# Attention scores in full precision on four row groups, units in pairs, in a four-batch layer on one core

## The chip, the cores and the metric

The kernel runs on one NeuronCore of a Trainium2 chip. TensorE (PE in the profile) multiplies matrices and writes to PSUM; VectorE (DVE), ScalarE (ACT) and GpSimd (POOL) do the elementwise work; SyncE (SP) issues DMAs. Each engine runs its own instructions in program order, and the engines wait for each other by semaphores. The metric is the device time of one execution in microseconds, lower is better.

## The reference, cut to what matters

x is 4 batches of 512 tokens by 256 features. Each batch goes through a conditioned down/up projection with a residual (h), an attention over 8 heads, and a gated expert layer behind a second conditioned projection. The attention is what the change touches:

```
paths = sigmoid(h @ Wp + bp)                    # 512 x 8 heads x 5 levels
agree = pq * pk + (1 - pq) * (1 - pk)           # query, key
sim   = cumprod(agree, -1).sum(-1) / 5
attn  = softmax(where(causal, sim, -inf), -1)
ctx   = attn @ (h @ Wv);   out = ctx @ Wo
x     = x + out
x     = x + ffn(cond2(x))                       # argmax over 8 experts, each a 256 x 256 matrix
```

With s = tanh(logit / 2) for a path's sign, the sum of running products is an inner product of 32 features per token and head (all 32 products of subsets of the 5 levels, each scaled by a constant). So a head's score is a matmul with a contraction of 32.

## The kernel before, in words

Everything is held transposed: features in partitions, tokens along the free axis. The order of all work is one list, ORDER. Each engine walks the same list and issues its own part of each step, so the list sets the order on every queue. A step that uses a PSUM bank gets one from `work` (two banks in the loop, six in the prologue, four of them borrowed from `s_ps`), and waits until the last user has emptied it.

The steps: `gdn`, `gup` (conditioned weights), `down`, `up` (h), `VL` (values and logits, four blocks of 128 tokens), `feat` (the 32 features, built on VectorE by doubling), `phi` (transposes of the features, 4 heads x 32 features in 128 partitions, two groups g of four heads), `U`, `Uadd`, `WoU`, `Q`, `G` (weights of the expert layer, once), then per batch `zT`, `zs` (expert input and scores, and the choice of an expert on VectorE), `zo` (choice times input), `zoT` (its transposes), `out` (four quarter outputs).

The attention of a batch is 12 units: for each group of four heads, query blocks 0 to 255 (units of 256 and 128 queries) and 256 to 511 (three of 256, one of 128), by key block of 128. A unit is: scores (four matmuls, one a head, into half a PSUM bank each, `s_ps`, two buffers), exp on ScalarE into `prob` (a ring of four), a causal mask on GpSimd where the block lies on the diagonal, and `context` (four matmuls into 32 output partitions each, `c_ps`). The sums of exp come from matmuls with ones, in the first half of the queries by unit; in the second half VectorE first adds the key blocks up (`tiles`, line 553), and one step `den` makes the matmuls. VectorE then normalises: a reciprocal and a product (lines 445 and 446). In the list a step `unit u` is context(u) and scores(u+2).

The scores before are made of half-precision parts. In `phi` ScalarE writes the high half of the scaled features three times (lines 405, 407, 408) and VectorE the rest in half precision twice (495, 499). Sixteen DMAs a batch (line 307, in the first batch eight of them on ScalarE's queue, line 414) then stack high and low parts of a head in four row groups, so that one half-precision matmul with a contraction of 128 gives the four products. `scores` of a batch waits for all sixteen (`stacked`).

Of the kernel before, what the change touches and what calls it, by code (L numbers as in the profile page):

```python
# [30 lines left out]
UNITS = [(g, *u) for chunk in (((0, 0, 256, True, False), (1, 128, 128, True, True)),  # L31
                               ((0, 256, 256, False, False), (1, 256, 256, False, False), (2, 256, 256, True, False),
                                (3, 384, 128, True, True))) for g in range(NG) for u in chunk]
BU = len(UNITS)
ALL = B * BU
# [1 line left out]
RING = 4
LONG = 4


def unit(u):

    return u // BU, UNITS[u % BU]


def diagonals(u):

    return sum(unit(i)[1][4] for i in range(u + 1))


def chunks(u):

    return sum(unit(i)[1][5] for i in range(u + 1))


def place(u):

    first = u
    while first % BU and not unit(first - 1)[1][5]:
        first -= 1  # L60
    return chunks(u) - unit(u)[1][5], u - first
# [771 lines left out]
```

## Time and profile before

| | us |
|---|---|
| median of 3 runs (lowest to highest) | 193.39 (192.97 to 193.41) |
| the profiled execution | 193.25 |
| its span, first to last instruction | 191.3 |
| PE busy in the span | 153.5 (80%) |
| VectorE busy | 110.8 (58%) |
| ScalarE busy | 70.8 (37%) |
| GpSimd busy | 25.3 (13%) |

Busy is the time in which an engine has at least one instruction under way. One full-precision matmul appears as two MATMUL records and two LDWEIGHTS records. The difference of 1.95 us between the profiled execution and its span is start and end outside the instructions.

### The profile page before, as it was taken

What the parts mean: (1) busy time and instruction counts of PE and PEld (TensorE: products, weight loads), DVE (VectorE), ACT (ScalarE), POOL (GpSimd) and SP (SyncE); (2) the same over time, 40 slices, a digit from 0 to 9 for tenths busy, and PEclk for the clock granted to TensorE, in tenths of its full rate; (3) what the DMA queues carried; (4) which work ended last, traced back from release to release, by engine and by line L of the source; (5) the groups of instructions that cost most, each with busy time, mean ns of one, the idle gap of its engine ahead of it and who ended that gap; (6) DMA issues with size and microseconds to landing.
All of it is one profiled execution on the core that took longest, in us unless ns stands there. A gap on an engine that the chain in (4) does not pass through costs nothing.

```text
span 191.3 us, 3377 instructions
## 1 busy us (share of the span) xinstructions
PE 153.5 (80%) x1326; PEld 90.4 (47%) x1326; DVE 110.8 (58%) x212; ACT 70.8 (37%) x110; POOL 25.3 (13%) x60
## 2 busy tenths in 40 slices
PE   0889839938799989659968999459849695999894
PEld 0346414414454535426545565244436362767573
DVE  0453952450887938995933466973901679476641
ACT  2003430323945453883512256660421364341010
POOL 7000000002203142020112110300202202020000
PEclk9999997985999999996999999975979998799999
DMA  5999899921068300007660000008840000001101
GB/s 144 305 416 381 365 362 254 252 47 26 3 156 205 83 0 3 0 0 165 159 175 27 31 0 3 0 0 192 195 114 27 27 3 0 6 26 55 48 35 55
DMA packets 12496, 20.78 MB, mean 109 GB/s; under 512 B 2576, under 2 KB 6832, under 8 KB 12352
## 3 DMA queue, kind: packets, MB, share of 16 engines
q1 hardware_dynamic: 9248, 12.24, 24.5%
q10 hardware_dynamic: 3136, 8.28, 12.6%
q0 software_dynamic: 96, 0.05, 0.6%
q8 instruction: 10, 0.16, 0.4%
q14 instruction: 6, 0.05, 0.1%
HBM read 9.95 MB, written 2.22 MB: 64 GB/s over the span
## 4 chain that ended last, share of the span: by engine, by line
PE 48%; DVE 26%; SPq 11%; issue 5%; DMA 5%; ACT 4%; POOL 1%; ACTq 0%; DVEq 0%
PE work L607 22%; PE s_ps L607 13%; SPq L307 11%; PE c_ps L607 10%; DVE rden L445 7%; DVE tiles L553 3%; DVE feat L598 3%; DMA st<-feat_h 3%; DVE feat_h L495 3%; DMA first_sb<-in_first 2%; DVE h_t L480 2%; PE work L777 2%; ACT prob L377 1%; DVE zo L580 1%; DVE ctx_t L446 1%
## 5 line engine op out<-in xcount | busy, mean ns | idle before, releaser
L377 ACT ACTIVATE prob<-s_ps 128x1024 f32<-128x1024 f32 (+1 forms) x48 | 41.9, 881 | 53.9 <-PE s_ps L607 51.5
L358 POOL TENSOR_SCALAR_AFFINE_SELECT prob<-prob 128x512 f32<-128x512 f32 x32 | 21.5, 677 | 145.6 <-ACT prob L377 145.6
L445 DVE RECIPROCAL rden<-c_ps 128x256 f32<-128x256 f32 x16 | 28.1, 1756 | 10.9 <-PE c_ps L607 10.8
L607 PE MATMUL s_ps<-st 128*128 128x256 f16 (+1 forms) x192 | 28.1, 274 | 7.2 <-DMA st<-feat_h 4.8
L607 PE MATMUL c_ps<-prob,v_sb 128*32 128x256 f32 (+1 forms) x384 | 28.9, 373 | 4.9 <-POOL prob L358 3.2
L607 PEld LDWEIGHTS s_ps<-st 128*128 128x128 f16 x192 | 14.4, 102 | 26.2 <-issue 16.9
L587 DVE TENSOR_TENSOR x_t<-work,x_t 128x256 f32<-128x256 f32 x16 | 6.8, 423 | 28.0 <-PE work L607 28.0
L607 PE MATMUL work<-ctx_t,mix_sb 128*128 128x256 f32 x64 | 19.9, 440 | 1.5 <-DVE h_t L480 0.8
L607 PE MATMUL work<-zo_t,gexp 128*128 128x256 f32 x64 | 17.6, 399 | 0.0
L607 PE MATMUL work<-w_vl,h_t 128*128 128x296 f32 x44 | 13.5, 430 | 4.1 <-DVE h_t L480 4.1
L553 DVE TENSOR_TENSOR tiles<-tiles,prob 128x1024 f32<-128x1024 f32 (+1 forms) x16 | 15.7, 980 | 1.8 <-POOL prob L358 1.8
L607 PEld LDWEIGHTS c_ps<-prob,v_sb 128*32 128x32 f32 x384 | 8.4, 111 | 16.1 <-POOL prob L358 7.6
L607 PEld LDWEIGHTS work<-ctx_t,mix_sb 128*128 128x128 f32 x64 | 12.8, 222 | 4.6 <-DVE h_t L480 1.2
L607 PEld LDWEIGHTS work<-zo_t,gexp 128*128 128x128 f32 x64 | 13.0, 204 | 2.2 <-ACT zo_t L427 0.2
L390 ACT COPY v_sb<-work 128x256 f32<-128x256 f32 x11 | 4.1, 373 | 26.3 <-DVE logit L489 17.9
L607 PEld LDWEIGHTS work<-w_vl,h_t 128*128 128x128 f32 x44 | 7.5, 190 | 8.0 <-issue 5.9
L777 PE MATMUL work<-ident,zo 128*128 128x128 f32 x32 | 6.1, 321 | 6.2 <-DVE zo L580 3.6
L553 DVE TENSOR_TENSOR tiles<-prob 128x1024 f32<-128x1024 f32 x8 | 10.2, 1278 | 0.5 <-ACT prob L377 0.5
L607 PE MATMUL c_ps<-prob,ones 128*32 128x128 f32 (+1 forms) x128 | 8.9, 351 | 0.0
L427 ACT COPY zo_t<-work 128x512 f32<-128x512 f32 x8 | 4.7, 586 | 11.3 <-PE work L777 11.0
L495 DVE SCALAR_TENSOR_TENSOR feat_h<-work,rootc,feat_h 128x512 f16<-128x512 f32 x6 | 4.5, 746 | 7.2 <-ACT feat_h L405 7.2
L777 PEld LDWEIGHTS work<-ident,zo 128*128 128x128 f32 x32 | 3.9, 160 | 8.8 <-issue 6.0
(105 smaller groups left out, 162.6 us busy)
## 6 DMA issues: line engine op xcount, KB each, us to landing
st<-feat_h SPq DMA_DIRECT2D x56, 128.0 KB, 2.5
wdec<-in_W_dec ACTq DMA_DIRECT2D x1, 3855.0 KB, 14.2
x_t<-in_x_tr SPq DMA_DIRECT2D x4, 512.0 KB, 8.7
ex_t<-in_expert_tr ACTq DMA_DIRECT2D x1, 2048.0 KB, 24.2
out_x<-x_t SPq DMA_DIRECT2D x16, 128.0 KB, 1.7
st<-feat_h ACTq DMA_DIRECT2D x8, 128.0 KB, 6.3
mix_sb<-in_mix ACTq DMA_DIRECT2D x1, 776.0 KB, 16.0
lift_sb<-in_lift ACTq DMA_DIRECT2D x1, 384.0 KB, 4.3
```

The source lines that it names most:

```text
L307: sp.dma_start(st[NF * q:NF * (q + 1), b % 2, :, h, :], feat_h[NF * h:NF * (h + 1), :, T * pair:T * (pair + 2)]).then_inc(stacked[b], 16)
L358: nc.gpsimd.affine_select(out=tri, in_=tri, compare_op=ALU.is_ge, fill=0.0, base=0, pattern=[[0, HG], [1, P]], channel_multiplier=-1).then ...
L377: nc.scalar.activation(prob[:, u % RING, :, 0:n], s_ps[:, u % 2, :, 0:n], ACT.Exp).then_inc(exped, 1)
L390: nc.scalar.copy(v_sb[:, b % 2, t, :], bank(s)[:, 0:D]).then_inc(empty(s), 1)
L427: nc.scalar.copy(zo_t[:, :, CW * s[2]:CW * (s[2] + 1)], bank(s)[:].rearrange("p (e t) -> p e t", e=2)).then_inc(empty(s), 1)
L445: link(nc.vector.reciprocal(rden[:], c_ps[m % 2][:, CW:2 * CW]))
L495: nc.vector.scalar_tensor_tensor(out=slots[:, 2, :], in0=bank(s)[:], scalar=rootc[:], in1=slots[:, 0, :], op0=ALU.mult, op1=ALU.subtract). ...
L553: nc.vector.tensor_tensor(acc, other, prob[:, v % RING, :, 0:n], ALU.add).then_inc(added, 1)
L587: nc.vector.tensor_tensor(x_t[:, b, c, half], bank(s)[:, 0:CW], x_t[:, b, c, half], ALU.add).then_inc(empty(s), 1)
L598: ins = nc.vector.tensor_tensor(feat[:, :, n:2 * n], feat[:, :, 0:n], sign[:, :, i:i + 1].broadcast_to([P, TT * H, n]), ALU.mult)
L607: return nc.tensor.matmul(o, w, r, start=start, stop=stop, skip_group_check=True)
L777: ins = nc.tensor.transpose(o[:, CW * e + P * i:CW * e + P * (i + 1)], zo[:, 2 * hf + i, 4 * e:4 * e + 4, :].rearrange("p e k -> p (e k)") ...
```

## The change

- The features stay in full precision. `phi` is the transposes and one scaled copy on ScalarE into `phi_t` (128 partitions = 4 heads x 32 features). The half-precision copies, the VectorE subtraction and copy, and all the stacking DMAs go.
- A head's score is a full-precision matmul with a contraction of 32, whose operands lie in partitions 32h to 32h+31; the four heads use four row groups of the array, and write to four different PSUM banks.
- Units go in pairs: 6 a batch (24 in all). `s_ps` is one buffer of four whole banks, one a head; exp, mask and semaphores are by pair, `prob` has two buffers of a pair. The list now has scores(p+1), some steps, context(p), `den` where a long chunk ends, more steps, and then `adds(p+1)` on VectorE.
- The first scores come right behind the first batch's `phi`; `down` and `up` of batch 1, its `VL`, and `U`, `Q`, `G` move behind it, between the pairs.
- `VL` is emptied by one ScalarE copy (values and logits); the bias is one VectorE instruction for four blocks (`bias`), and tanh is a step of its own.
- `zo` of batches 0 to 2 moves from VectorE to GpSimd.
- Nine matmuls on the identity matrix run on TensorE before its first step.

The core of the diff:

```diff
+PAIRS = [(g, 0, ((0, 0, 256), (1, 128, 128)), True, True, True) for g in range(NG)]
+for _g in range(NG):
+    PAIRS += [(_g, 1, ((0, 256, 256), (1, 256, 256)), False, True, False),
+              (_g, 1, ((2, 256, 256), (3, 384, 128)), True, False, True)]
...
+            ("gup", 2), ("gup", 3), ("phi", 0, 0), ("phi", 0, 1), ("scores", 0), ("down", 1)]
...
+        gaps[2] += [("zs", prv, ALL_T), ("zo", prv, 0), ("zo", prv, 1)]
+    if b >= 1 and n1 < B:
+        gaps[2] += [("bias", n1), ("tanh", n1), ("feat", n1)]
...
+        _p = _b * BP + _i
+        if _p + 1 < ALL:
+            ORDER += [("scores", _p + 1)]
+        ORDER += _a + [("context", _p)]
+        if PAIRS[_i][1] and PAIRS[_i][5]:
+            ORDER += [("den", chunk(_p))]
+        ORDER += _c
+        if _p + 1 < ALL:
+            ORDER += [("adds", _p + 1)]
...
-        feat_h = sb("feat_h", [P, NG, 5 * T], F16)
-        st = sb("st", [P, 2, NG, HG, 2 * T], F16)
-        prob = sb("prob", [P, RING, HG, CW])
+        phi_t = sb("phi_t", [P, 2, NG, T])
+        prob = sb("prob", [P, 2, HG, ROWS])
-        s_ps = ps("s_ps", [P, 2, HG, CW])
+        s_ps = ps("s_ps", [P, HG, ROWS])
...
-                    sp.wait_ge(copies_ready, NG * (b + 1))
-                    sp.wait_ge(halves_ready, NG * (b + 1))
-                    if b >= 2:
-                        sp.wait_ge(scored, BU * (b - 1))
-                    for q, pair in SLOTS[:2] if b == 0 else SLOTS:
-                        for h in range(HG):
-                            sp.dma_start(st[NF * q:NF * (q + 1), b % 2, :, h, :],
-                                         feat_h[NF * h:NF * (h + 1), :, T * pair:T * (pair + 2)]
-                                         ).then_inc(stacked[b], 16)
...
+                    tri = prob[:, p % 2].rearrange("p h (s q) -> p h s q", s=2)[:, :, :, 0:P]
+                    nc.gpsimd.affine_select(out=tri, in_=tri, compare_op=ALU.is_ge, fill=0.0, base=0,
+                                            pattern=[[0, HG], [0, 2], [1, P]], channel_multiplier=-1
+                                            ).then_inc(masked, 1)
+                elif s[0] == "zo" and s[1] < B - 1:
+
+                    _, b, hf = s
+                    done(pool, ("zs", b, ALL_T))
+                    for t in (2 * hf, 2 * hf + 1):
+                        ins = nc.gpsimd.tensor_tensor(zo[:, t], z_nat[:, t:t + 1, :].broadcast_to([P, E, KP]),
+                                                      pick[:, t, :].unsqueeze(2).broadcast_to([P, E, KP]), ALU.mult)
+                    ins.then_inc(zo_ready, 1)
...
+                if s[0] == "scores":
+                    p = s[1]
+                    act.wait_ge(scored, p + 1)
+                    if p >= 2:
+                        act.wait_ge(summed, p - 1)
+                        if adds(p - 2):
+                            act.wait_ge(added, adds(p - 2))
+                    nc.scalar.activation(prob[:, p % 2, :, 0:width(p)], s_ps[:, :, 0:width(p)], ACT.Exp
+                                         ).then_inc(exped, 1)
...
+                    nc.scalar.copy(v_sb[:, b % 2, t, :], bank(s)[:, 0:D + H * DEPTH]).then_inc(empty(s), 1)
...
-                    nc.scalar.activation(slots[:, 0, :], bank(s)[:], ACT.Copy, scale=rootc[:]).then_inc(high_ready, 1)
-                    act.wait_ge(high_ready, NG * b + g + 1)
-                    nc.scalar.copy(slots[:, 1, :], slots[:, 0, :])
-                    nc.scalar.copy(slots[:, 4, :], slots[:, 0, :]).then_inc(copies_ready, 1)
-                    if b == 0 and g == NG - 1:
-                        act.wait_ge(copies_ready, NG)
-                        act.wait_ge(halves_ready, NG)
-                        for q, pair in SLOTS[2:]:
-                            for h in range(HG):
-                                act.dma_start(st[NF * q:NF * (q + 1), b % 2, :, h, :],
-                                              feat_h[NF * h:NF * (h + 1), :, T * pair:T * (pair + 2)]
-                                              ).then_inc(stacked[b], 16)
+                    nc.scalar.activation(phi_t[:, b % 2, g, :], bank(s)[:], ACT.Copy, scale=rootc[:]
+                                         ).then_inc(empty(s), 1)
...
+                elif kind == "bias":
+                    b = s[1]
+                    if b == 0:
                         dve.wait_ge(ld_bp, 16)
-                        if b >= 1:
-                            dve.wait_ge(sign_ready, b)
-                    full(dve, s)
-                    nc.vector.tensor_tensor(logit[:, t, :], bank(s)[:, D:D + H * DEPTH], bp_b[:], ALU.add
+                    else:
+                        dve.wait_ge(sign_ready, b)
+                    done(dve, ("VL", b, TT - 1))
+                    nc.vector.tensor_tensor(logit[:], v_sb[:, b % 2, :, D:],
+                                            bp_b[:].unsqueeze(1).broadcast_to([P, TT, H * DEPTH]), ALU.add
                                             ).then_inc(logit_ready, 1)
...
-                    nc.vector.scalar_tensor_tensor(out=slots[:, 2, :], in0=bank(s)[:], scalar=rootc[:],
-                                                   in1=slots[:, 0, :], op0=ALU.mult, op1=ALU.subtract
-                                                   ).then_inc(empty(s), 1)
-                    done(dve, s)
-                    nc.vector.tensor_copy(slots[:, 3, :], slots[:, 2, :]).then_inc(halves_ready, 1)
...
+                    if half:
+                        both = prob[:, p % 2].rearrange("p h (s q) -> p h s q", s=2)
+                        acc = tiles[:, chunk(p) % 2]
+                        if first:
+                            dve.wait_ge(exped, p + 1)
+                            nc.vector.tensor_tensor(acc, both[:, :, 0, :], both[:, :, 1, :], ALU.add
+                                                    ).then_inc(added, 1)
+                        else:
+                            dve.wait_ge(masked, masks(p))
+                            dve.wait_ge(added, adds(p) - 2)
+                            nc.vector.tensor_tensor(acc, acc, both[:, :, 0, :], ALU.add).then_inc(added, 1)
+                            dve.wait_ge(added, adds(p) - 1)
+                            nc.vector.tensor_tensor(acc[:, :, P:CW], acc[:, :, P:CW], both[:, :, 1, 0:P], ALU.add
+                                                    ).then_inc(added, 1)
...
+                    pe.wait_ge(exped, p)
+                if p % BP < NG:
+                    done(pe, ("phi", b, g))
+                for i, (kt, q0, n) in enumerate(units):
+                    for h in range(HG):
+                        rows = slice(NF * h, NF * (h + 1))
+                        ins = mm(s_ps[:, h, CW * i:CW * i + n], phi_t[rows, b % 2, g, P * kt:P * (kt + 1)],
+                                 phi_t[rows, b % 2, g, q0:q0 + n])
...
+            for _ in range(WARM):
+                mm(c_ps[0][:, 0:P], ident[:], ident[:])
```

On TensorE, the end of the prologue. Before, from the weights `gup` of batches 2 and 3 to the first scores (`s_ps<-st`); `work<-x_t,w_dn` is `down`, `<-act_t,w_up` is `up`, `<-w_vl,h_t` is `VL`, `<-wdec` is `U`:

```order
L607 MATMUL work<-x_t,w_dn 64x256 x4
L717 MATMUL s_ps<-ident,feat 128x128 x8
L607 MATMUL s_ps<-act_t,w_up 128x256 x4
L607 MATMUL work<-w_vl,h_t 128x296 x2
L607 MATMUL work<-wdec,first_sb 32x480 x4
...
L607 MATMUL work<-wdec,first_sb 32x30
L607 MATMUL s_ps<-mix_sb 128x8 x2
L607 MATMUL s_ps<-ex_t,mix_sb 32x256 x8
L607 MATMUL s_ps<-st 128x256 x4
L607 MATMUL s_ps<-st 128x128 x4
```

And now, from the same `gup`:

```order
L585 MATMUL work<-lift_sb,cond_b 128x512 x2
L697 MATMUL s_ps<-ident,feat 128x128 x8
L585 MATMUL s_ps<-phi_t 128x256 x4
L585 MATMUL s_ps<-phi_t 128x128 x4
L585 MATMUL work<-x_t,w_dn 64x256 x4
L585 MATMUL s_ps<-phi_t 128x256 x4
L585 MATMUL s_ps<-phi_t 128x128 x4
L585 MATMUL work<-act_t,w_up 128x256 x4
L585 MATMUL c_ps<-prob,v_sb 32x256 x4
```

The scores stand directly behind the transposes, and `down` and `up` of batch 1 behind them; its `VL` and the `U` steps come later, among the pairs.

On VectorE, in the attention of batch 1, around the choice of an expert (`z_nat` to `pick`) and the features of batch 2 (`feat`). Before:

```order
L565 COPY z_nat<-work 128x128
L567 TENSOR_REDUCE smax<-work 128x4
L568 TENSOR_TENSOR hit<-work,smax 128x32
L570 TENSOR_TENSOR key<-hit,rank 128x32
L571 TENSOR_REDUCE kmax<-key 128x4
L572 TENSOR_TENSOR pick<-key,kmax 128x32
L553 TENSOR_TENSOR tiles<-prob 128x1024
L495 SCALAR_TENSOR_TENSOR feat_h<-work,rootc,feat_h 128x512
L499 COPY feat_h<-feat_h 128x512
L580 TENSOR_TENSOR zo<-z_nat,pick 128x256 x2
L553 TENSOR_TENSOR tiles<-tiles,prob 128x1024
```

And now:

```order
L523 TENSOR_TENSOR tiles<-prob 128x1024
...
L549 TENSOR_REDUCE kmax<-key 128x4
L550 TENSOR_TENSOR pick<-key,kmax 128x32
L474 TENSOR_TENSOR logit<-v_sb,bp_b 128x160
L573 COPY feat<-sign 128x32
L576 TENSOR_TENSOR feat<-feat,sign 128x32x2
L576 TENSOR_TENSOR feat<-feat,sign 128x32x4
L576 TENSOR_TENSOR feat<-feat,sign 128x32x8
L576 TENSOR_TENSOR feat<-feat,sign 128x32x16
L528 TENSOR_TENSOR tiles<-tiles,prob 128x1024
L530 TENSOR_TENSOR tiles<-tiles,prob 128x4x128
```

The choice, the bias and the features of the next batch now stand in one row ahead of the additions (lines 528 and 530) that close the first long chunk.

## Rows read from the trace of the kernel before

**Rows 1.** The page, busy time, share of the span and instructions of an engine.
```profile
PE 153.5 (80%) x1326; PEld 90.4 (47%) x1326; DVE 110.8 (58%) x212; ACT 70.8 (37%) x110; POOL 25.3 (13%) x60
```

**Rows 2.** The chain that ended last, share of the span by line.
```profile
PE work L607 22%; PE s_ps L607 13%; SPq L307 11%; PE c_ps L607 10%; DVE rden L445 7%; DVE tiles L553 3%; DVE feat L598 3%; DMA st<-feat_h 3%; DVE feat_h L495 3%; DMA first_sb<-in_first 2%; DVE h_t L480 2%; PE work L777 2%; ACT prob L377 1%; DVE zo L580 1%; DVE ctx_t L446 1%
```

**Rows 3.** Waits of TensorE: us in total, times, longest.
```profile
PE work L607 <- DVE h_t L480: 4.9, 3, 3.5
PE s_ps L607 <- DMA st<-feat_h: 4.8, 2, 3.1
```

**Rows 4.** Cores: span, mean granted TensorE clock.
```profile
core 0: 191.3 us, clock 0.929
```

**Rows 5.** Timeline, prologue: start, us, engine, line, shapes, count, [idle before <-releaser].
```profile
19.43 1.74 DVE L598 TENSOR_TENSOR feat<-feat,sign 128x64 f32<-128x64 f32 x4
...
21.32 1.06 PE L717 MATMUL s_ps<-ident,feat 128*128 128x128 f32 x8 [0.48 <-DVE feat L598]
...
25.69 8.62 SPq L307 DMA_DIRECT2D st<-feat_h  x8
...
26.94 1.31 PE L607 MATMUL work<-w_vl,h_t 128*128 128x296 f32 x4 [3.49 <-DVE h_t L480]
...
41.18 1.05 PE L607 MATMUL s_ps<-st 128*128 128x256 f16 x8 [2.48 <-DVE gexp L531]
```

**Rows 6.** Matmuls on one tile: duration in ns, minimum/median/maximum, first and last start.
```profile
L607 PE MATMUL s_ps<-x_t,w_dn x8: 634/634/689, 7.7 to 9.0; 128*64 128x256 f32 x8
L607 PE MATMUL work<-x_t,w_dn x8: 379/379/430, 19.8 to 20.5; 128*64 128x256 f32 x8
```

**Rows 7.** Timeline of TensorE in the attention of batch 0.
```profile
55.22 0.64 PE L607 MATMUL c_ps<-prob,v_sb 128*32 128x256 f32 x8
55.80 0.61 PE L607 MATMUL s_ps<-st 128*128 128x256 f16 x4
56.34 1.08 PE L607 MATMUL work<-x_t,w_dn 128*64 128x256 f32 x8
...
57.92 0.40 PE L607 MATMUL s_ps<-st 128*128 128x128 f16 x4
58.25 0.64 PE L607 MATMUL c_ps<-prob,v_sb 128*32 128x256 f32 x8
...
59.36 1.14 PE L607 MATMUL work<-act_t,w_up 64*128 64x256 f32 x8
60.43 0.32 PE L607 MATMUL c_ps<-prob,v_sb 128*32 128x128 f32 x4
```

**Rows 8.** Groups by line and shape: count | busy us, mean ns | idle before.
```profile
L377 ACT ACTIVATE prob<-s_ps 128x1024 f32<-128x1024 f32 x32 | 32.8, 1024 | 47.8 <-PE s_ps L607 45.5 <-DVE tiles L553 2.1
...
L358 POOL TENSOR_SCALAR_AFFINE_SELECT prob<-prob 128x512 f32<-128x512 f32 x32 | 21.5, 677 | 145.6 <-ACT prob L377 145.6
...
L553 DVE TENSOR_TENSOR tiles<-tiles,prob 128x1024 f32<-128x1024 f32 x8 | 10.2, 1276 | 0.6 <-POOL prob L358 0.6
L377 ACT ACTIVATE prob<-s_ps 128x512 f32<-128x512 f32 x16 | 9.5, 597 | 6.1 <-PE s_ps L607 6.1
...
L580 DVE TENSOR_TENSOR zo<-z_nat,pick 128x256 f32<-128x256 f32 x16 | 6.0, 418 | 0.1
L553 DVE TENSOR_TENSOR tiles<-tiles,prob 128x512 f32<-128x512 f32 x8 | 5.5, 684 | 1.2 <-POOL prob L358 1.2
...
L395 ACT ACTIVATE sign<-logit 128x160 f32<-128x160 f32 x4 | 1.4, 340 | 0.0
```

**Rows 9.** Timeline of VectorE in the attention of batch 1.
```profile
81.58 0.28 DVE L565 COPY z_nat<-work 128x128 f32<-128x128 f32 x1
...
83.14 0.19 DVE L572 TENSOR_TENSOR pick<-key,kmax 128x32 f32<-128x32 f32 x1
```

**Rows 10.** Timeline, after a wait in batch 1.
```profile
86.28 1.09 PE L777 MATMUL work<-ident,zo 128*128 128x128 f32 x4 [2.19 <-DVE zo L580]
```

**Rows 11.** Stretches: busy us of each engine (count), granted clock, DMA share, GB/s.
```profile
86.00:89.40 3.40, 3.12 (x18) 2.16 (x19) 2.54 (x5) 1.03 (x2) 0.00 (x0) 0.50 0.68 157
```

More of the change, by code:

```diff
@@ L27, with pair, chunk, width @@
 U_PIECE = U_COLS // 4
[L31 to L35, printed above, removed]
-BC = 2 * NG
[L37 to L61, printed above, removed]
+ROWS = 2 * CW
+WARM = 9
+PAIRS = [(g, 0, ((0, 0, 256), (1, 128, 128)), True, True, True) for g in range(NG)]
+for _g in range(NG):
+    PAIRS += [(_g, 1, ((0, 256, 256), (1, 256, 256)), False, True, False),
+              (_g, 1, ((2, 256, 256), (3, 384, 128)), True, False, True)]
+BP = len(PAIRS)
+ALL = B * BP
+BC = 2 * NG
+def pair(p):
+    return p // BP, PAIRS[p % BP]
+def chunk(p):
+    return sum(pair(i)[1][5] for i in range(p))
+def width(p):
+    return sum(n for _, _, n in pair(p)[1][2])
+def masks(p):
+    return sum(pair(i)[1][3] for i in range(p + 1))
 def long(m):
@@ new lines, in after_scores @@
+def after_scores(b):
+    n1, prv = b + 1, b - 1
+    gaps = [[] for _ in range(BP)]
+    if n1 < B:
+        gaps[0] += [("up", n1, 0), ("up", n1, 1)]
+    if b == 0:
+        gaps[1] += [("VL", n1, 2), ("VL", n1, 3)]
+        gaps[2] += [("U", 1)]
+        gaps[3] += [("U", 3)]
+        gaps[4] += [("Q",), ("Uadd",)]
+        gaps[5] += [("G", 1)]
+    elif n1 < B:
+        gaps[1] += [("VL", n1, 0), ("VL", n1, 1)]
+        gaps[2] += [("VL", n1, 2), ("VL", n1, 3)]
+    if b == 1:
+        gaps[0] += [("WoU",)]
+    if prv >= 1:
+        gaps[0] += [("out", prv - 1, 3)]
+    if prv >= 0:
+        gaps[4] += [("zoT", prv, 1)]
+        gaps[5] += [("out", prv, 1)]
+    return gaps
@@ L132, in between @@
     return gaps
 ORDER = list(PROLOGUE)
-_open = []
 for _b in range(B):
-    for _i, _gap in enumerate(between(_b)):
-        _u = _b * BU + _i
-        ORDER += [("unit", _u)] + _open
-        _m = place(_u)[0]
-        _open = [("den", _m)] if UNITS[_i][5] and long(_m) else []
-        ORDER += _gap
-ORDER += _open + [("out", B - 1, 0), ("zT", B - 1, SECOND), ("zs", B - 1, SECOND), ("zo", B - 1, 1),
-                  ("out", B - 1, 1), ("zoT", B - 1, 1), ("out", B - 1, 2), ("out", B - 1, 3)]
@@ L147 @@
-SLOTS = ((0, 0), (1, 1), (2, 3), (3, 2))
-NO_BANK = ("unit", "den", "start", "Uadd", "feat", "zo")
+    for _i, (_a, _c) in enumerate(zip(after_scores(_b), after_context(_b))):
+        _p = _b * BP + _i
[7 more added lines that the diff above has]
+            ORDER += [("adds", _p + 1)]
+ORDER += [("out", B - 1, 0), ("zT", B - 1, SECOND), ("zs", B - 1, SECOND), ("zo", B - 1, 1),
+          ("out", B - 1, 1), ("zoT", B - 1, 1), ("out", B - 1, 2), ("out", B - 1, 3)]
@@ L149 @@
+NO_BANK = ("scores", "context", "den", "adds", "bias", "tanh", "feat", "Uadd", "zo")
 EARLY = 6
-WORK, _turns = {}, [0] * EARLY
+WORK, _turns, _late = {}, [0] * EARLY, 0
 for _n, _s in enumerate(s for s in ORDER if s[0] not in NO_BANK):
-    _k = _n % (EARLY if _s in PROLOGUE else 2)
+    if _s in EARLY_BANK:
+        _k = EARLY_BANK[_s]
+    else:
+        _k, _late = _late % 2, _late + 1
     WORK[_s] = (_n, _k, _turns[_k])
     _turns[_k] += 1
-EARLY_TURNS = [1 + max(turn for _, k, turn in WORK.values() if k == i) for i in range(EARLY)]
+EARLY_TURNS = [sum(k == i for k in EARLY_BANK.values()) for i in range(EARLY)]
@@ L296, in _ @@
             for s in ORDER:
[L297 to L310 removed]
+                if s == ("U", 3):
                     done(sp, s)
```

224 lines of the change are left out of this document (78 added, 146 removed), and 3 rows, old and new, of the table PROLOGUE.

## The prediction

> **What bounds the kernel now.** I read the shares first: TensorE is busy 153.5 of 191.3 us, VectorE 110.8 [rows 1]. No engine is full, so the kernel is TensorE's work plus what it waits for. The chain of waits says for what: beside TensorE's own lines, SyncE's queue with the stacking DMAs (line 307) holds 11% of the span and their landing 3%; VectorE's reciprocals, feature products and half-precision parts hold 7, 3 and 3% [rows 2]. TensorE's waits name the same places: 4.8 us on the stacking, 4.9 us on h [rows 3]. In the prologue the first features are transposed at 21.32 us, but the first scores start at 41.18 us [rows 5]. Last the clock: the mean grant is 0.929 [rows 4]. A clock of either 1.2 or 2.4 GHz gives this mean with 0.142 of the span, 27.2 us, at the lower level.
>
> I split the span so: 37.8 us without a matmul (191.3 less 153.5), and in the 153.5 a surcharge for the low clock. A stretch at half clock was busy 3.12 of 3.40 us [rows 11], so some 25 of the 27.2 us were work, of which half, 12.5 us, is surcharge. At the start the granted clock shows nothing, but a `down` matmul takes 634 ns there and 379 later [rows 6], so another 2.8 us of the 5.6 us from 5.3 to 10.9 is surcharge. Work at full clock: 153.5 - 15.3 = 138.2 us.
>
> **Scores on four row groups.** Columns now: 0.54 us for a half-precision unit of 256 queries (56.34 less 55.80), 0.33 for 128 (58.25 less 57.92) [rows 7], so 0.21 us per 128 columns and four heads, and 0.12 fixed. Full precision needs two records of a doubled stream for each matmul: a `context` unit of 256, four heads in four column groups, takes 0.58 us for eight records (55.80 less 55.22) [rows 7], which is possible only if the four groups run beside each other. Row groups have one witness, `up`: its two halves use 64 rows each, and eight records take 1.07 us (60.43 less 59.36) [rows 7]; one after the other they would take 4 x 0.43 = 1.7. A pair of 512 columns is four records in each of four groups, the same depth as `up`. At full overlap it takes 1.07 us, the two units it replaces 1.08. So scores cost what they did. That four groups overlap as two do isn't in the trace. Bounds: nothing lost; or no overlap, where 2560 columns a head and batch in four passes at 2.4 GHz are 68.3 us for 4 heads and 4 batches instead of a quarter, 17.1, that is +51.2 us. I take nothing lost, next to the nearest row.
>
> The Trainium skill ("TensorE: Matmul & The Clock Gate", Part 3) reports a measured 3.07 times for four row groups, not 4. By that figure the scores would take 68.3/3.07 = 22.2 us, 5 us more than in my sum. No row here has four row groups.
>
> **Pairs.** Where two units of one kind stand together one fixed part goes: 24 contexts and 8 `den` at 0.13 are -4.2 us of TensorE. Exp of a pair: by the two shapes, 597 and 1024 ns [rows 8], 0.17 fixed and 0.83 per 1000 elements, so 1.45 us (1536 elements) and 1.88 (2048); `scores(p+1)` must wait for it. Between the end of one scores and the next stand other steps of 2 to 5 us in most places, so this hides; in the first pair, with only `down` (1.07) there, it costs 0.4. A mask of twice the size is some 1.1 us (677 ns before [rows 8]; bounds 0.68 and 1.35) and has the next scores (0.85 to 1.07) to hide behind.
>
> **What goes.** The stack, 32 half-precision copies and the SyncE queue cost the path three times: before the first scores, and before batches 2 and 3 (rows 3 has the 4.8). On ScalarE and VectorE the copies are cover elsewhere, as neither engine is full. `zo` on GpSimd instead of VectorE: 12 of 16 at 418 ns [rows 8] leave VectorE, 5.0 us; on GpSimd no product is seen: between VectorE's 0.4 and twice its own mask of 512 elements, 1.35; I take 0.7, as the mask is the nearest row. The first half has two pairs' steps to hide behind, the second one pair more, so up to 1.35 nothing waits.
>
> **Prologue.** It stays a chain down, up, h, VL, tanh, feat, phi. Nine matmuls on the identity fill 1.6 to 5.5 us, so the clock should rise about 3.4 us earlier than the 10.9 that the start implies: 1.7 us won. The bias behind all four copies costs 0.1. Then transposes at 19.7 us (21.32 before [rows 5]), two copies of the features, and the first scores at 21.8, 19.4 us earlier than 41.18. Of that, 11.8 us is work that moves among the pairs and still has to be done. TensorE idles 3.8 us between its first matmul and these scores (h, features, copies).
>
> **The loop.** Now TensorE meets VectorE's queue. In batches 1 and 2 the order has the choice (81.58 to 83.33, 1.75 us [rows 9]), bias (0.3, estimate by shape), tanh (0.34 [rows 8]), features (a copy of 0.2 and 1.74 [rows 5]) and the two additions (1.28 and 0.68 [rows 8]) in one row ahead of the first long `den`: 6.4 us with the hand-overs. Behind the expert scores TensorE has only scores(p+1) (1.07) and a context (0.8) to do. So it waits 4.5 us, twice. In batch 3, without features, 1.35, and 1.5 before the second `den`, with 1.0 at the end as before. In batch 0 the `U` copies share VectorE with features and additions: 1.4 and 0.85; the weights' way through memory holds VectorE in `Uadd`, and so `G`: 1.05, 1.7 and 0.5; with the 0.4 above 5.9. The sum: 5.9 + 4.5 + 4.5 + 3.9 = 18.8 us of waits.
>
> The clock: a wait of 2.19 us at 84 to 86.28 [rows 10] was followed by 3.4 us at half clock [rows 11]. The two long waits should each bring one such stretch, batch 0 one, the prologue one: 4 x 1.5 = 6.0, and 1.1 at the start.
>
> **The sum.** Work 138.2 - 4.2 = 134.0; before the first step 5.3; behind the last matmul 2.6; prologue 3.8; loop 18.8; gaps under 0.25 us 2.6 as now; low clock 7.1. Together 174.2 us of span against 191.3, and with 1.95 us outside it 176.2. The profiled execution (193.25) is 0.14 under the median of the runs, so 176.3; I say 176.
>
> **Rivals.**
> A, the VectorE row doesn't bind: TensorE reaches the long `den` late anyway, because all else is slower than I have it. Without the two waits of 4.5 and their stretches of low clock: 176.3 - 9 - 3 = 164. For it: VectorE loses `zo` (5.0 us) and the half-precision rest, so it comes to the row earlier. Against: the order of instructions, which leaves TensorE 1.9 us to cover 6.4.
>
> B, the small buffers bind: exp of p waits for the additions of p-2 and stands behind tanh in ScalarE's queue, and the next scores wait for exp. Now, with a ring of four and two score buffers, ScalarE already waits 2.1 us for `tiles` [rows 8]. If it costs 0.6 us in each of 18 pairs: +11, 187 us.
>
> C, the other side, slower: the row groups don't run beside each other. The scores then take 68.3/n us at n groups at a time. The change has 17 us to give back by the other terms, so it breaks even where 68.3/n = 17.1 + 17.1, at n = 2.0. At two at a time 193, at one 176 + 51 = 227. For it: no row shows four; that `up`'s halves overlap, and the four column groups do, speaks against.
>
> **Chances.** Forecast 176 (170 to 183) 0.60; A 0.15; B (183 to 191) 0.15; C 0.10, of which two thirds slower than now. The range to hold it 8 times in 10 leaves the slow end of B and C out, and the fast tail of A: 166 to 187. A measurement of this kernel can tell about 0.3%, 0.6 us, from no change. Faster 0.91, within 0.3% 0.02, slower 0.07.
>
> **What would show it.** In the profile after: eight records or sixteen of `s_ps<-phi_t` in about 0.85 to 1.1 us from the start of one pair to the next step (C if 1.9 or more). First exp near 22.7 us. No DMA between the prologue and the outputs but the weights'. A wait of 4 to 5 us of TensorE in batches 1 and 2 ahead of `c_ps<-tiles`, released by `tiles` on VectorE (A if under 1). ScalarE waiting for TensorE, not for `tiles` or the bias (B otherwise). Low clock in four stretches of the loop, against eight now, a mean grant near 0.96. The forecast is wrong if TensorE's waits in the loop are under 12 or over 26 us.

## The result, and the profile after

| | before | after |
|---|---|---|
| median, us (lowest to highest, runs) | 193.4 (192.97 to 194.88, 4) | 177.47 (176.12 to 178.64, 4) |
| profiled execution / its span, us | 193.25 / 191.3 | 177.1 / 175.0 |
| mean granted TensorE clock | 0.929 | 0.971 |

The ratio is 0.916, 95% interval 0.908 to 0.925: the kernel is 8.4% faster. The forecast was 176 (166 to 187), by a span of 174.2. Here and below a median is over all runs of a kernel, while ratios and their intervals leave out the runs that fell in a slower state of the chip.

The busy shares of the page after answer to [rows 1], the second fence to the cores' row of [rows 4]:

```profile
PE 145.8 (83%) x1536; PEld 98.0 (56%) x1536; DVE 99.6 (57%) x172; ACT 59.3 (34%) x70; POOL 30.6 (18%) x56
```

```profile
core 0: 175.0 us, clock 0.971
```

TensorE is busy 145.8 us, 7.7 less, though 4.0 us of it are the new matmuls on the identity. It is without a matmul for 29.2 us instead of 37.8. The chain of waits after, by line, answers to [rows 2]:

```profile
PE work L585 30%; PE c_ps L585 16%; PE s_ps L585 12%; DVE feat L576 4%; DVE tiles L528 3%; DVE rden L430 3%; PE work L757 3%; DMA u_scratch<-u_row 2%; PE work L697 2%; DVE tiles L523 2%; DVE tiles L530 2%; DVE h_t L465 2%; DMA u_raw<-u_scratch 1%; DVE u_row L491 1%; ACT prob L375 1%
```

The stack has left it, and SyncE's queue keeps 1% of it; VectorE's features and additions (`tiles`, now lines 523, 528, 530) stand in their place. TensorE's waits, against [rows 3] (us in total, times, longest):

```profile
PE c_ps L585 <- DVE tiles L530: 12.6, 5, 4.9
PE work L585 <- DVE ub_col L495: 3.3, 1, 3.3
PE work L585 <- DVE u_row L491: 2.2, 1, 2.2
PE work L585 <- DVE h_t L465: 2.1, 3, 0.8
...
PE s_ps L585 <- ACT prob L375: 0.6, 1, 0.6
```

The prologue on TensorE, against [rows 5] (start, us, engine, line, shapes, records, idle before and its releaser):

```profile
1.59 4.21 PE L585 MATMUL c_ps<-ident 128*128 128x128 f32 x18 [1.59 <-POOL ident L326]
...
19.60 1.06 PE L697 MATMUL s_ps<-ident,feat 128*128 128x128 f32 x8 [1.68 <-DVE feat L576]
21.65 0.94 PE L585 MATMUL s_ps<-phi_t 32*128 32x256 f32 x16 [0.98 <-ACT phi_t L400]
22.52 1.08 PE L585 MATMUL work<-x_t,w_dn 128*64 128x256 f32 x8
```

The first scores, sixteen records for 256 and 128 queries, start at 21.65 us and hold TensorE until 22.52: 0.87 us. Later in the loop, a pair of 512 columns goes from 64.55 to 65.63, 1.08 us:

```profile
64.55 1.15 PE L585 MATMUL s_ps<-phi_t 32*128 32x256 f32 x16
65.63 2.26 PE L585 MATMUL work<-w_vl,h_t 128*128 128x296 f32 x8
```

The groups by shape that answer to [rows 8] (count | busy us, mean ns | idle before):

```profile
L375 ACT ACTIVATE prob<-s_ps 128x1536 f32<-128x1536 f32 x16 | 23.2, 1450 | 17.2 <-PE s_ps L585 17.1
...
L352 POOL TENSOR_SCALAR_AFFINE_SELECT prob<-prob 128x1024 f32<-128x1024 f32 x16 | 18.3, 1146 | 115.6 <-ACT prob L375 115.6
...
L375 ACT ACTIVATE prob<-s_ps 128x2048 f32<-128x2048 f32 x8 | 15.0, 1873 | 16.3 <-PE s_ps L585 13.4 <-DVE tiles L523 2.9
...
L360 POOL TENSOR_TENSOR zo<-z_nat,pick 128x256 f32<-128x256 f32 x12 | 8.5, 738 | 5.2 <-DVE pick L550 5.2
```

And the place of the two long waits, VectorE in the attention of batch 1, against [rows 9]:

```profile
74.70 0.29 DVE L543 COPY z_nat<-work 128x128 f32<-128x128 f32 x1 [1.95 <-PE work L585]
...
75.91 0.32 DVE L474 TENSOR_TENSOR logit<-v_sb,bp_b 128x160 f32<-128x160 f32 x1
76.62 0.20 DVE L573 COPY feat<-sign 128x32 f32<-128x32 f32 x1 [0.40 <-ACT sign L393]
76.86 2.64 DVE L576 TENSOR_TENSOR feat<-feat,sign 128x64 f32<-128x64 f32 x4
79.42 1.22 DVE L528 TENSOR_TENSOR tiles<-tiles,prob 128x1024 f32<-128x1024 f32 x1
80.67 0.69 DVE L530 TENSOR_TENSOR tiles<-tiles,prob 128x512 f32<-128x512 f32 x1
82.23 1.76 DVE L430 RECIPROCAL rden<-c_ps 128x256 f32<-128x256 f32 x1 [0.87 <-PE c_ps L585]
```

From 74.70 to 81.36 VectorE's row lasts 6.7 us, with one pause of 0.40 us for tanh, and TensorE waits for its end: `den` starts at 81.42 after 4.89 us without a matmul. GpSimd makes its products beside the features:

```profile
81.42 0.77 PE L585 MATMUL c_ps<-tiles,ones 128*32 128x256 f32 x8 [4.89 <-DVE tiles L530]
```

```profile
76.07 2.42 POOL L360 TENSOR_TENSOR zo<-z_nat,pick 128x256 f32<-128x256 f32 x4 [2.32 <-DVE pick L550]
```

Behind this wait the clock is low, as after the wait in [rows 10, 11] (busy us of each engine, granted clock, DMA):

```profile
76.50:81.80 5.30, 0.41 (x12) 0.16 (x8) 4.57 (x7) 1.86 (x2) 1.99 (x4) 1.00 0.00 0
81.80:85.20 3.40, 3.40 (x24) 2.54 (x20) 2.94 (x3) 1.41 (x3) 0.00 (x0) 0.50 0.00 0
```

### The profile page after: what moved, and what is told of

The parts are those of the page before. It is cut to its first block, busy times and chain, and to the rows that moved or that the text cites. A ratio compares the mean times of both kernels' runs of the same rounds, so it can differ in the third digit from the quotient of the medians.

```text
span 175.0 us, 3582 instructions
## 1 busy us (share of the span) xinstructions
PE 145.8 (83%) x1536; PEld 98.0 (56%) x1536; DVE 99.6 (57%) x172; ACT 59.3 (34%) x70; POOL 30.6 (18%) x56
## 3 DMA queue, kind: packets, MB, share of 16 engines
q1 hardware_dynamic: 4768, 4.89, 8.6%
## 4 chain that ended last, share of the span: by engine, by line
PE 64%; DVE 23%; issue 4%; DMA 4%; ACT 3%; SPq 1%; POOL 0%; POOLq 0%; DVEq 0%; ACTq 0%
PE work L585 30%; PE c_ps L585 16%; PE s_ps L585 12%; DVE feat L576 4%; DVE tiles L528 3%; DVE rden L430 3%; PE work L757 3%; DMA u_scratch<-u_row 2%; PE work L697 2%; DVE tiles L523 2%; DVE tiles L530 2%; DVE h_t L465 2%; DMA u_raw<-u_scratch 1%; DVE u_row L491 1%; ACT prob L375 1%
## 5 line engine op out<-in xcount | busy, mean ns | idle before, releaser
L375 ACT ACTIVATE prob<-s_ps 128x1536 f32<-128x1536 f32 (+1 forms) x24 | 38.2, 1591 | 33.5 <-PE s_ps L585 30.5
L352 POOL TENSOR_SCALAR_AFFINE_SELECT prob<-prob 128x1024 f32<-128x1024 f32 x16 | 18.3, 1146 | 115.6 <-ACT prob L375 115.6
L585 PE MATMUL s_ps<-phi_t 32*128 32x256 f32 (+1 forms) x384 | 24.2, 366 | 1.5 <-ACT phi_t L400 1.0
L585 PE MATMUL c_ps<-prob,v_sb 128*32 128x256 f32 (+1 forms) x384 | 24.4, 358 | 0.0
L585 PEld LDWEIGHTS s_ps<-phi_t 32*128 32x128 f32 x384 | 17.5, 186 | 9.3 <-issue 5.6
L585 PE MATMUL c_ps<-tiles,ones 128*32 128x256 f32 x64 | 5.8, 437 | 12.6 <-DVE tiles L530 12.6
L528 DVE TENSOR_TENSOR tiles<-tiles,prob 128x1024 f32<-128x1024 f32 x8 | 9.7, 1216 | 0.0
L360 POOL TENSOR_TENSOR zo<-z_nat,pick 128x256 f32<-128x256 f32 x12 | 8.5, 738 | 5.2 <-DVE pick L550 5.2
L576 DVE TENSOR_TENSOR feat<-feat,sign 128x64 f32<-128x64 f32 (+3 forms) x16 | 8.3, 522 | 0.5
L465 DVE TENSOR_TENSOR h_t<-work,x_t 128x512 f32<-128x512 f32 x6 | 3.9, 686 | 8.1 <-PE work L585 8.1
```

Source lines behind the costliest of these rows:

```text
L352: nc.gpsimd.affine_select(out=tri, in_=tri, compare_op=ALU.is_ge, fill=0.0, base=0, pattern=[[0, HG], [0, 2], [1, P]], channel_multiplier= ...
L360: ins = nc.gpsimd.tensor_tensor(zo[:, t], z_nat[:, t:t + 1, :].broadcast_to([P, E, KP]), pick[:, t, :].unsqueeze(2).broadcast_to([P, E, KP ...
L375: nc.scalar.activation(prob[:, p % 2, :, 0:width(p)], s_ps[:, :, 0:width(p)], ACT.Exp).then_inc(exped, 1)
L465: nc.vector.tensor_tensor(h_t[:, :, half], bank(s)[:].rearrange("p (c t) -> p c t", c=DC), x_t[:, b, :, half], ALU.add).then_inc(empty(s), 1)
L528: nc.vector.tensor_tensor(acc, acc, both[:, :, 0, :], ALU.add).then_inc(added, 1)
L576: ins = nc.vector.tensor_tensor(feat[:, :, n:2 * n], feat[:, :, 0:n], sign[:, :, i:i + 1].broadcast_to([P, TT * H, n]), ALU.mult)
```

## The experiments

Times are medians in us. "Before" was 193.5 to 194.6 on the chips of these runs.

### Do the row groups run beside each other?

```diff
-                        rows = slice(NF * h, NF * (h + 1))
+                        rows = slice(0, NF)                              # one_group
+                        rows = slice(NF * (h // 2), NF * (h // 2 + 1))   # two_groups
```

> All four heads' score matmuls use the first row group (partitions 0 to 31 of phi_t); same count, shapes and banks, so the scores computed are those of one head of four. Theory (the four groups run beside each other): a pair of 512 columns goes from 1.08 us to about 3.5, one of 384 from 0.87 to 2.7; 8 and 16 of them make +49 us of TensorE work, of which some 7 us fall into waits that are there now, so 215 to 226 us. Rival (the groups never mattered, something else overlaps the records): under +20 us.

> Heads 0 and 1 on the first row group, 2 and 3 on the second; scores of two heads are computed twice. Theory: a pair of 512 takes about 1.95 us, one of 384 about 1.5, in all +17 us of work, 3 of it in present waits: 189 to 194 us, that is no gain over the kernel before, the break-even of the prediction. Rival (two groups already fill some shared limit, so four give little more): under 183.

Measured: one group 233.37 (ratio to before 1.206, 1.200 to 1.213), two groups 192.96 (0.998, 0.994 to 1.002). The first score step of each, with the step behind it; two groups first, then one:

```profile
21.88 1.68 PE L585 MATMUL s_ps<-phi_t 32*128 32x256 f32 x16 [0.98 <-ACT phi_t L400]
23.49 1.08 PE L585 MATMUL work<-x_t,w_dn 128*64 128x256 f32 x8
```

```profile
21.51 3.60 PE L585 MATMUL s_ps<-phi_t 32*128 32x256 f32 x16 [0.98 <-ACT phi_t L400]
25.04 1.98 PE L585 MATMUL work<-x_t,w_dn 128*64 128x256 f32 x8
```

The same sixteen records take 0.87 us on four groups, 1.61 on two and 3.53 on one (the last partly at the low clock). At the full clock, later in the loop, a step of 384 columns takes 2.81 us on one group (47.37 to 50.18), and one of 512 takes 3.64 (83.20 to 86.84); on two groups the longer one takes 2.03 (66.97 to 69.00):

```profile
47.37 2.88 PE L585 MATMUL s_ps<-phi_t 32*128 32x256 f32 x16
50.18 1.28 PE L585 MATMUL work<-wdec,first_sb 128*32 128x480 f32 x8
...
83.20 3.71 PE L585 MATMUL s_ps<-phi_t 32*128 32x256 f32 x16
86.84 2.26 PE L585 MATMUL work<-w_vl,h_t 128*128 128x296 f32 x8
```

So 128 columns more of four heads cost 0.83 us on one group, 0.42 on two and 0.21 on four, and a whole step, with its fixed part, goes 3.2 to 3.4 times as fast on four groups as on one. Four groups do overlap, and the whole gain hangs on it: at two it is gone, as the prediction's break-even of n = 2.0 has it. One group missed its range of 215 to 226 by 7 us, and its clock says why: mean grant 0.882. TensorE is busy 215.6 us, 69.9 more than in the change. By the mean grants the low clock is some 27 us of the busy time, against 5 in the change, so the work itself grew by 48 us (an estimate), as expected. Its profile has two stretches of 13.7 us at the low level. The first begins during the first scores, 2.0 us behind a wait of 0.98. The second begins inside a wait of 2.3 us for `tiles` and lasts on through score steps on a single group:

```profile
153.20:166.90 13.70, 11.99 (x56) 8.24 (x56) 4.94 (x5) 4.41 (x6) 1.09 (x1) 0.50 0.00 1
168.00:180.00 12.00, 12.00 (x79) 9.30 (x78) 5.19 (x7) 1.73 (x2) 1.10 (x1) 1.00 0.09 33
```

### Does the order of the matmuls matter?

```diff
-                for i, (kt, q0, n) in enumerate(units):
-                    for h in range(HG):
+                for h in range(HG):
+                    for i, (kt, q0, n) in enumerate(units):
```

> The score matmuls of a pair are issued head by head (both units of head 0, then of head 1) instead of unit by unit. Theory (a matmul starts when its row group is free, whatever stands ahead of it in other groups, as the two halves of `up` do): same time, 176.5 to 178.5 us, score steps still 0.87 and 1.08. Rival (matmuls start strictly in program order, so only neighbours on different groups overlap): a pair of 512 takes some 3 us, +30 us or more.

Measured 177.41 (0.917, 0.913 to 0.921), as the change itself. A score step takes 0.89 us (22.07 to 22.96) instead of 0.87. The records of the first step that have started by 22.30 us are four. In one_group it is one by 21.80, 0.29 us from the step's start:

```profile
22.07 0.52 PE L585 MATMUL s_ps<-phi_t 32*128 32x256 f32 x4 [0.98 <-ACT phi_t L400]
```

```profile
21.51 0.48 PE L585 MATMUL s_ps<-phi_t 32*128 32x256 f32 x1 [0.98 <-ACT phi_t L400]
```

Head by head, three more records of the first head stand ahead of the second head's first one. In strict program order one record would have started by then. The theory stands: a matmul doesn't wait for those ahead of it in other row groups.

### The matmuls on the identity

```diff
-WARM = 9
+WARM = 0
```

> The nine matmuls on the identity ahead of the first step are left out (they feed nothing). Theory: the clock rises about 3.4 us later, at 10 to 11 us, and the prologue up to the first scores gets 1.0 to 2.5 us longer; nothing changes behind it: 178.5 to 180. Rival (the prologue is bound by DMAs and VectorE, the clock is free): within 0.5 us.

Measured 179.78 (0.930, 0.926 to 0.934), 2.4 us over head_major, which ran on the same chip with the same time as the change. `down` without and with the nine, and the transposes behind; first without:

```profile
7.25 1.98 PE L585 MATMUL s_ps<-x_t,w_dn 128*64 128x256 f32 x8
...
20.73 1.06 PE L697 MATMUL s_ps<-ident,feat 128*128 128x128 f32 x8 [1.68 <-DVE feat L576]
```

```profile
7.32 1.08 PE L585 MATMUL s_ps<-x_t,w_dn 128*64 128x256 f32 x8
```

`down` takes half as long at the same place, and the transposes start at 19.60 instead of 20.73. The profiles show 1.1 us of the medians' 2.4; the rest may be where the low stretches fall behind it, which wasn't separated.

### VectorE's row ahead of the additions

```diff
-        gaps[2] += [("bias", n1), ("tanh", n1), ("feat", n1)]
+        gaps[3] += [("bias", n1), ("tanh", n1), ("feat", n1)]
-        gaps[3] += [("phi", n1, 0), ("phi", n1, 1)]
+        gaps[4 if b else 3] += [("phi", n1, 0), ("phi", n1, 1)]
```

> In batches 1 and 2 bias, tanh and features of the next batch move behind the first long `den`, its transposes one pair further. Theory (VectorE's row ahead of the additions makes the two waits of 4.9 us): 2.7 us of the row go, each wait falls to about 2, and the low clock behind them goes too: 168 to 172 us. Rival A (the waits move to the transposes or to the second long `den` instead): 175 or more.

Measured 172.73 (0.890, 0.882 to 0.898), 4.7 us less than the change by the medians and 5.0 by the ratios. The two waits fell to 1.67 us each, 6.4 us less in all; a wait for the transposes came (2.0 us in two places, released by `x_t` on VectorE):

```profile
PE c_ps L585 <- DVE tiles L530: 5.4, 4, 1.7
...
PE work L697 <- DVE x_t L565: 2.0, 2, 1.7
```

The theory holds for the waits; each fell by 3.2 us, more than the row's 2.7, and all features take 1.74 us here, no longer beside GpSimd's products. The gain is short of the range's slow end by 0.7 us (0.2 by the ratio), by part of rival A. That the low clock behind the waits goes too isn't shown by this profile: its mean grant is 0.951, with a low stretch behind one of the shorter waits (of 1.67 us, at 79.8). The other three runs have 0.979 to 0.990.

```diff
-                elif kind == "zo" and s[1] == B - 1:      # VectorE
+                elif kind == "zo":
-                elif s[0] == "zo" and s[1] < B - 1:       # GpSimd
+                elif s[0] == "zo" and s[1] < 0:
```

> The products `zo` of batches 0 to 2 go back from GpSimd to VectorE. Theory (VectorE's row is on the path in batches 1 to 3): the four products, 1.7 us, stand ahead of the additions in each of three batches: +4 to +6, 181 to 183 us. Rival (they only take VectorE's slack): within 1 us.

Measured 179.66 (0.927, 0.919 to 0.935): +2.2, under half of what was expected. Each long wait grew by 0.6 us only, and the one of batch 3 from 1.12 to 2.29:

```profile
PE c_ps L585 <- DVE tiles L530: 14.6, 5, 5.5
```

So VectorE's queue is on the path there, but not with all of the 1.7 us. The rest is in the features. The products take 1.43 us on VectorE, and the features behind them 1.74, where they took 2.64 with GpSimd's products beside them:

```profile
74.88 1.43 DVE L558 TENSOR_TENSOR zo<-z_nat,pick 128x256 f32<-128x256 f32 x4
...
77.17 1.74 DVE L576 TENSOR_TENSOR feat<-feat,sign 128x64 f32<-128x64 f32 x4
```

The row is 1.46 us longer and 0.90 shorter, in all 0.56, which is the growth of each long wait. In batch 3 there are no features; there the last addition went from 0.99 to 0.69 us, and the wait grew by 1.17. So moving `zo` to GpSimd is worth only part of what it takes off VectorE: while GpSimd multiplies, VectorE's features are slower. In adds_first, where they start after GpSimd's products, they take 1.74 us again.

### Uadd

```diff
-        gaps[4] += [("Q",), ("Uadd",)]
+        gaps[4] += [("Q",)]
...
+    if b == 0:
+        gaps[5] += [("Uadd",)]
```

> `Uadd`, which holds VectorE until the expert weights are back from memory, moves behind the last `den` of batch 0. Theory: the wait of 3.3 us ahead of the second `G` goes (the copy behind which it stands is done at once) and with it a stretch of low clock, -3 to -5 us: 172 to 175. Rival (the hold only covers a wait for exp and additions that comes anyway): within 1 us.

Measured 174.0 (0.896, 0.889 to 0.903), -3.5. The wait released by `ub_col` (3.3 us) is gone, all others stand as they did: the theory, in size too. The clock gave nothing back in this profile (mean grant 0.959): the low stretch behind `ub_col` is gone, but those at the two long waits last 6.8 us each instead of 3.4.

### All of it

all_three is feat_later and uadd_later together, and has `U`'s first three copies on ScalarE:

```diff
+                elif s[0] == "U" and s[1] < 3:            # ScalarE
+                    m = s[1]
+                    full(act, s)
+                    nc.scalar.copy(u_row[:, U_PIECE * m:U_PIECE * (m + 1)], bank(s)[:, 0:U_PIECE]
+                                   ).then_inc(empty(s), 1)
```

> feat_later and uadd_later together, and three of the four copies of `U` on ScalarE instead of VectorE. Theory: -7 from the features, -4 from Uadd, -2.5 from the wait of 2.2 us for a bank of `U` and the 0.7 behind it: 161 to 166 us. Rival (VectorE's load binds in other places): above 169.

Measured 166.64 (0.858, 0.852 to 0.865), 0.6 above the range. adds_first has all of this and changes the order once more:

```diff
-        ORDER += _c
+        if _i != 2:
+            ORDER += _c
         if _p + 1 < ALL:
             ORDER += [("adds", _p + 1)]
+        if _i == 2:
+            ORDER += _c
...
-        gaps[3] += [("zoT", prv, 0)]
-        gaps[4] += [("zoT", prv, 1)]
+        gaps[4] += [("zoT", prv, 0), ("zoT", prv, 1)]
```

> all_three, with the additions of the first long chunk ahead of the choice of an expert in the order, and both `zoT` behind the next pair's scores. Theory (the 1.7 us that TensorE still waits twice for the additions, and 1.1 once, are the choice's 1.75 us): these waits go, some wait for `zo` may come, 161 to 165 us. Rival (VectorE's load, not its order, binds by now): within 1 us of all_three's 166.6.

Measured 163.44 (0.847, 0.841 to 0.853), within its range, the best kernel of this study and 7.9% under the change. Its clock, and its waits for `tiles`:

```profile
core 0: 161.4 us, clock 1.000
```

```profile
PE c_ps L596 <- DVE tiles L541: 3.0, 3, 1.5
```

VectorE still does 97.3 us of work (99.6 in the change): mostly order, not load, made the waits, as feat_later, which moves no work between engines, shows by itself. With no wait over 1.7 us behind the start, the granted clock doesn't fall once. That isn't a rule: all_three, whose waits in the loop are 1.67 us at most, has one low stretch:

```profile
82.34:85.70 3.36, 3.36 (x12) 2.19 (x14) 0.18 (x2) 1.26 (x1) 1.10 (x1) 0.50 0.00 0
```

### The stack, and the work in front

```diff
-                    for q, pair in SLOTS[:2] if b == 0 else SLOTS:
+                    for q, pair in SLOTS[:2] if b == 0 else ():              # before_no_stack
+                    for q, pair in SLOTS if b == 1 else SLOTS[:2]:           # half_stack
```

(with the waits' counts to match, and all scores of before_no_stack reading `st[:, 0]`)

> The kernel before, without the stacking DMAs of batches 1 to 3; their scores read the stack of batch 0, so they are wrong by content, same by shape. Theory (the stack costs the loop only the waits of 1.7 and 3.1 us for it and a stretch of low clock): 186 to 189 us, so under half of the gain. Rival (what the chain shows, 11% and 3% of the span on its queue and landing, is its price): 170 to 178.

> The kernel before, with eight stacking DMAs instead of sixteen for batches 2 and 3 (the two upper row groups keep the parts of two batches ago, so those scores are wrong by content). Theory (the stack costs by lateness, 0.65 us of issue each on SyncE's queue behind the last features, 10 us in all, so that the scores of the next batch and the outputs behind it wait): eight end 5 us earlier, before the scores need them, and nearly the whole price of the loop's stack goes, 181 to 185 us. Rival (the price is in the number of transfers and the waits they share with other work): about half of it, 186 to 189.

Measured: without the stack 181.45 (0.941, 0.929 to 0.952), with half of it 182.23 (0.947, 0.938 to 0.955). The first theory fell: the stack in the loop costs the kernel before some 12 us (11.5 by the ratio), nearly three quarters of the size of the change's gain, not 5 to 7. The stretch of the loop in the kernel before, without and with half the stack, each to its end:

```profile
41.20:191.30 150.10, 124.59 (x1184) 75.88 (x1184) 91.36 (x157) 61.79 (x91) 21.52 (x32) 0.92 0.23 58
```

```profile
41.20:179.50 138.30, 118.81 (x1184) 72.88 (x1181) 90.76 (x157) 61.69 (x91) 22.69 (x32) 0.95 0.05 17
```

```profile
41.20:181.50 140.30, 120.93 (x1184) 74.24 (x1184) 90.99 (x157) 61.81 (x91) 22.70 (x32) 0.94 0.19 47
```

Of the 11.8 us, 6.0 are time without a matmul (25.5 to 19.5) and 5.8 busy time of the very same 1184 records; by the grants in these rows (0.92 and 0.95) the low clock is 5.1 of it. I had counted one low stretch of 1.5 us for two waits; in this pair of profiles the price of a wait was about twice its length. The half stack shows what about the stack it was. The issue of the DMAs before, and then with half:

```profile
85.53 11.58 SPq L307 DMA_DIRECT2D st<-feat_h  x16
```

```profile
85.65 5.95 SPq L307 DMA_DIRECT2D st<-feat_h  x8
```

```profile
99.15 0.61 PE L607 MATMUL s_ps<-st 128*128 128x256 f16 x4 [1.67 <-DMA st<-feat_h]
```

Of sixteen DMAs issued one by one, the last is issued at 97.1 us, and its data is there at 99.15, where the scores were due at 97.5. Of eight the last is issued at 91.6, and the scores start at 97.68 without a wait. Eight transfers fewer in each of batches 2 and 3, with all sixteen left in batch 1, take away 10 of the 11.5 us (by the ratios; 9.8 of 11.8 by the spans): the price was for the most part the lateness of the last one, not the traffic.

```diff
-            ("gup", 2), ("gup", 3), ("phi", 0, 0), ("phi", 0, 1), ("scores", 0), ("down", 1)]
+            ("gup", 2), ("gup", 3), ("phi", 0, 0), ("phi", 0, 1), ("down", 1), ("up", 1, 0), ("up", 1, 1),
+            ("VL", 1, 0), ("VL", 1, 1), ("U", 0), ("VL", 1, 2), ("U", 1), ("VL", 1, 3), ("U", 2), ("bias", 1),
+            ("tanh", 1), ("U", 3), ("feat", 1), ("Q",), ("G", 0), ("scores", 0)]
```

> The changed kernel with the work that was moved among the pairs (down, up, VL of batch 1, U, Q, the first G) back in front of the first scores. Theory (the early start of the scores wins by giving the pairs of batch 0 something to hide exp, mask and additions behind): first scores at 35 to 37 us, batch 0 then waits some 10 us, total +5 to +9: 182 to 186. Rival (the order of this work is neutral, the gain was in the stack alone): within 1.5 us of 177.5.

Measured 176.71 (0.913, 0.905 to 0.921): no slower at all. The theory fell, the rival stands. The first scores start at 34.10 us, 12.4 later, and batch 1 begins where it did (the `up` of batch 2, which stands at its start, at 59.80 against 60.12). In batch 0 TensorE waits 5.6 us, not 10, in eight short waits, while in the change the moved work brings waits of its own, 2.20 us for `U`'s bank and 3.26 behind `Uadd`, of 7.2 in all.

## Why the prediction was right

**The scores.** Priced as equal to the half-precision units, by `up` at 1.07 and four groups like two. Measured 0.87 and 1.08 us where 0.85 and 1.07 were said. The one step that nothing in the trace could show, four groups at a time, held, and one_group and two_groups show that it carries the result. (The 2560 columns "a head" are those of the two heads that share a row group; the 68.3 us are right.)

The Trainium skill ("TensorE: Matmul & The Clock Gate", Part 3) has 3.07 times for four row groups. The prediction set this against the columns alone; a step would then have been some 0.2 to 0.25 us longer (an estimate from 0.64 and 0.85 us of columns), and it isn't. Taken for a whole step the figure fits: 2.81 and 3.64 us on one group against 0.87 and 1.08 on four are 3.2 and 3.4 times. The columns overlap in full (0.83 against 0.21 us for 128), and the fixed part, which the prediction had counted already, makes the difference.

**The parts.** Exp 1450 and 1873 ns (1.45, 1.88 said), mask 1146 (1.1), `zo` on GpSimd 738 (0.7), first scores at 21.65 (21.8). The Trainium skill ("GPSIMD Engine Reference", section 3, "Performance versus the Vector engine") puts an addition of two inputs on GpSimd at about twice VectorE's time; the product here takes 738 against 418 ns, 1.8 times, and nothing waits long for it. What the prediction lacked is that VectorE's features beside it would take 2.64 us instead of 1.74.

**The waits.** The row on VectorE was to make two waits of 4.5 us, and made 4.89 and 4.88. It was to last 6.4 us and lasts 6.7, by two errors against each other: the choice takes 1.3 us and not 1.75, the features 0.9 more. Batch 3's waits were to be 1.35 and 1.5, and are 1.12 and 0.97. Two waits for `h_t` in batches 1 and 2, 0.77 us each, were left out. Batch 0's came out at 7.2 us, not 5.9: the wait for `U`'s bank is 2.20 where I had 1.4, and the wait behind `Uadd` is 3.26 where I had 1.7, as VectorE waits 4.2 us there for the weights to come back from memory. feat_later, uadd_later and adds_first show that these places are the cause.

**The sum**, term by term: full-clock work 136.2 (145.8 less 4.0 for the identity, 5.1 and 0.5 for the low clock) against 134.0; waits of the loop 21.5 against 18.8; prologue 3.3 against 3.8; small gaps 0.3 against 2.6; low clock 5.6 against 7.1 (three stretches instead of four, none from the prologue); start 5.6 (1.6 and the 4.0 of the identity) against 5.3; behind the last matmul 2.6 as said. The errors are +2.2, +2.7, -0.5, -2.3, -1.5 and +0.3, in all +0.9 with rounding: 175.0 for 174.2 us. It is closer than its terms, and that is luck. Two of them have a known cause. The 2.6 us of small gaps "as now" was a misreading: the gaps under 0.25 us in the trace of the kernel before add up to 0.2 us. And of the 2.2 us of work too many some 1.2 are the scores, which cost 22.6 us where the half-precision ones took 21.3 at the full clock, and 0.4 the pairs, which saved 3.8 us and not 4.2 (estimates from the records' starts and the granted clock).

**What the sum hid.** Where the gain came from I would have told wrongly. Asked on its own, I put the stack in the loop at 5 to 7 us and the early scores at 5 to 9; measured, 12 and nothing. The forecast didn't suffer since it summed the kernel after from its own work and waits, and never needed the difference of the two kernels by cause. No run has the pairs alone; the 3.8 us above is what can be said of them.

Rival A (164) was wrong: the row binds. That adds_first comes out at 163.4 is chance, since that kernel also loses the waits behind `Uadd` and for `U`. Rival B: ScalarE waits 2.9 us for `tiles`, against 2.1 before, but TensorE waits for exp only 0.6 us in all, not 0.6 in each of 18 pairs. Rival C is excluded by the score steps; its price of 193 us at two groups is what two_groups measured (192.96).

## What to carry to other kernels

- Where a list sets the order on every engine, write down for each step that TensorE will wait for what stands ahead of it in the other engine's queue, and compare with the work TensorE has until then. Here this gave two waits to 0.4 us, and moving such steps gave 14 us more, with VectorE's load nearly the same (97.3 us for 99.6).
- A chain of small DMAs issued one by one is priced by when the last one ends against when it is due. Halving the count in the two later batches took away most of it.
- Work moved to GpSimd isn't free for VectorE: look at what VectorE runs beside it. Here features of 1.74 us took 2.64.
- Full-precision matmuls with a contraction of 32 lose little against half-precision ones with 128 (some 1 us in 22 here) if four row groups are used together; at two groups the gain is gone. Here each group has a PSUM bank of its own; whether that is needed was not tried.

## What the runs showed of the hardware

- Matmuls in different row groups start without regard to program order: head by head or unit by unit, a score step takes 0.89 or 0.87 us, and the whole kernel the same time.
- Four heads' scores in full precision cost 0.21 us for each 128 columns on four row groups, 0.42 on two, 0.83 on one.
- While GpSimd runs products of two inputs (76.07 to 78.49 us), VectorE's feature products take 2.64 us; without them 1.74, in the same kernel for batches 0 and 1 (17.72 and 37.78 us), and everywhere in zo_vector, feat_later and adds_first. A mask on GpSimd beside the features (37.78 us) didn't change their time.
- The clock doesn't follow from the length of a wait alone. The change's waits of 3.26, 4.89 and 4.88 us each brought a low stretch of 3.4 us, its wait of 2.20 none. In no_warm the same wait of 2.2 us was followed by a stretch and the one of 3.26 by none. In head_major a wait of 4.87 brought 6.8 us. With loop waits of at most 1.7 us, adds_first has no stretch and all_three one. With the scores on one row group the low level once held 13.7 us, though TensorE was without a matmul for only 1.7 us of them, and a pair's scores took 5.4 us (158.76 to 164.18). Why it held so long was not tried.
